# Sparsemax attention: one row of candidates taken before the flag is read, TensorE's candidate rows in another order, and ten rotating rows of kept scores

## The reference

```python
def sparsemax(x):
    x = x - jnp.max(x, axis=-1, keepdims=True)
    zs = -jnp.sort(-x, axis=-1)
    rho = jnp.arange(1, L + 1, dtype=x.dtype)
    cssv = jnp.cumsum(zs, axis=-1) - 1.0
    support = zs > cssv / rho
    k = jnp.maximum(jnp.sum(support, axis=-1, keepdims=True), 1)
    tau = jnp.take_along_axis(cssv, k - 1, axis=-1) / k.astype(x.dtype)
    return jnp.clip(x - tau, 0.0)
```

## Time and profile before

| what | us |
|---|---|
| median of three runs (3720.1 to 3721.49) | 3720.78 |
| the profiled execution | 3726.95 |
| its span | 3725.1 |
| TensorE busy | 2808.6 (75%) |
| VectorE busy | 2231.3 (60%) |
| ScalarE busy | 1432.7 (38%) |
| first to last candidate MAX8, start | 875.5 to 1547.2 |
| first to last probability, start | 959.7 to 1640.6 |

### The profile page before, as it was taken

One profiled execution on the slowest core, in us unless ns is written; L12 is line 12 of the kernel. 1 busy time (PEld: TensorE's weight loads), 2 busy tenths in 40 slices (PEclk: granted clock), 3 DMA queues, 4 the chain that ended last, 5 costly groups with the idle time before them and its releaser, 6 DMA issues. The chain is left out here.

```text
span 3725.1 us, 39786 instructions
## 1 busy us (share of the span) xinstructions
PE 2808.6 (75%) x12862; PEld 1808.0 (49%) x12862; DVE 2231.3 (60%) x4947; ACT 1432.7 (38%) x2218; POOL 329.6 (9%) x145
## 2 busy tenths in 40 slices
PE   2999998354566666667999966888587696699588
PEld 2444445132233333336888844554443685354377
DVE  4666764865777677624555544656564555676377
ACT  2444442212787787732222212222143222166221
POOL 0000000020000000001212202011100110200021
PEclk8999999676777777768999978998888797799799
DMA  1000000024001111001111010000331010522010
GB/s 58 14 8 13 13 8 13 23 74 134 1 23 23 23 24 28 1 10 66 36 48 51 25 48 1 1 0 0 100 75 36 32 45 17 176 69 52 19 46 29
DMA packets 53741, 136.62 MB, mean 37 GB/s; under 512 B 8793, under 2 KB 29281, under 8 KB 48993
## 3 DMA queue, kind: packets, MB, share of 16 engines
q1 hardware_dynamic: 53600, 135.01, 12.2%
HBM read 106.28 MB, written 28.31 MB: 36 GB/s over the span
## 5 line engine op out<-in xcount | busy, mean ns | idle before, releaser
L1675 PE MATMUL ps<-m1e_x_part_s,m1e_up_part_s 128*128 128x512 f32 x1296 | 298.0, 391 | 22.0 <-POOL m1e_up_part_s L1771 15.9
L1445 ACT ACTIVATE l1a_over_s<-l1a_sc_s,l1a_minus_step_s 128x1024 bf16<-128x1024 f32 x256 | 290.0, 1139 | 3.0 <-DVE l1a_minus_step_s L1319 1.7
L1675 PEld LDWEIGHTS ps<-m1e_x_part_s,m1e_up_part_s 128*128 128x128 f32 x1296 | 243.8, 189 | 74.2 <-issue 23.7
L1259 DVE MAX8 l1a_cand_s<-ps 128x8 f32<-128x128 f32 x1024 | 213.0, 281 | 72.0 <-PE ps L1154 68.8
L1187 PE MATMUL ps<-l1a_probs_s,l1h_v_s 128*32 128x256 f32 x1024 | 126.5, 584 | 158.0 <-ACT l1a_probs_s L1453 156.5
L1431 ACT ACTIVATE l1a_sc_s<-ps,l1a_minus_tau_s 128x1024 f32<-128x1024 f32 x128 | 142.0, 1112 | 155.9 <-DVE l1a_minus_tau_s L1288 67.3
L1718 ACT ACTIVATE m1e_act_out_s<-ps 128x512 f32<-128x512 f32 x108 | 64.6, 598 | 346.8 <-PE ps L1675 346.8
L538 DVE TENSOR_SCALAR l0a_probs_s<-l0a_probs_s 128x1024 f32<-128x1024 f32 x128 | 88.4, 691 | 150.3 <-ACT l0a_probs_s L605 149.9
L974 DVE TENSOR_REDUCE l3a_shift_s<-ps 128x1 f32<-128x1024 f32 x128 | 150.3, 1219 | 46.1 <-PE ps L891 46.1
L605 ACT ACTIVATE l0a_probs_s<-ps 128x1024 f32<-128x1024 f32 x128 | 131.1, 1024 | 104.5 <-PE ps L455 103.3
L1154 PE MATMUL ps<-l1h_ka_s,l1h_qa_s 128*128 128x512 f32 x256 | 132.7, 564 | 49.7 <-DVE l1a_cand_s L1259 45.2
(11 more groups left out here) (530 smaller groups left out, 5873.9 us busy)
## 6 DMA issues: line engine op xcount, KB each, us to landing
m1ew_up_s<-m_up SPq DMA_DIRECT2D x9, 1536.0 KB, 6.2
l1h_ka_s<-l_k_parts SPq DMA_DIRECT2D x16, 512.0 KB, 8.0
l3h_ka_s<-l_k_parts SPq DMA_DIRECT2D x16, 512.0 KB, 8.1
m1ew_down_s<-m_down SPq DMA_DIRECT2D x9, 768.0 KB, 4.2
l0a_w_s<-l_w SPq DMA_DIRECT2D x16, 384.0 KB, 2.9
m3ew_up_s<-m_up SPq DMA_DIRECT2D x6, 768.0 KB, 4.2
l1h_qa_s<-l_q_parts SPq DMA_DIRECT2D x16, 256.0 KB, 6.0
l_v_groups<-l1p_v_all_s SPq DMA_DIRECT2D x8, 512.0 KB, 2.9
```

Of the source, the lines that this page charges most:

```text
L1259: ins = nc.vector.max(cand[:, r, 8 * (c + j * 4):8 * (c + j * 4) + 8], ps[:, A0 + f % 2, c * P:(c + 1) * P])
L1445: nc.scalar.activation(over[:, done % 2, :], sc[:, r, :], ACT.Relu, bias=minus_step[:, r:r + 1], accum_out=total[:, i, r:r + 1]).then_inc( ...
L1675: ins = nc.tensor.matmul(ps[:, 2 * (u % 2) + way, :], up_parts[a][:, k, way, c, :], x_parts[b][:, k, half * BANK:(half + 1) * BANK], start ...
```

## The change

Four things change in the stage.

1. **Ten rotating rows of kept scores.** Row r of unit u is kept in row (8u + r) mod 10. Rows 0 and 1 of the next unit then overwrite nothing that the loop behind the flag may read, and ScalarE waits for `settled` only at row 2 (`KEPT - ROWS`).
2. **One row of candidates ahead.** VectorE takes candidate row 0 of unit u + 2 in `settle(u)`, between the last step and the maximum of the worst excesses. So in the next turn rows 1 to 4 stand where rows 0 to 3 stood, and rows 5 to 7 where rows 4 to 7 stood. At the start row 0 of unit 1 is taken behind the first threshold of unit 0.
3. **TensorE's order.** `first_row` moves on by one place to match; row 0 of unit u + 2 stands behind the value products of t = 2.
4. **Three probability buffers instead of four.** A probability waits for the value products three places back.

```diff
+    KEPT = ROWS + 2
+    def kept(u, r):
+
+        return (ROWS * u + r) % KEPT
-        sc = s.sb("sc", [P, ROWS, nk])
+        sc = s.sb("sc", [P, KEPT, nk])
-        probs = s.sb("probs", [P, 4, 2 * NQ])
+        probs = s.sb("probs", [P, 3, 2 * NQ])
...
             for r in range(ROWS):
                 first_row(0, r)
+            first_row(1, 0)
...
                     if u + 1 < UNITS and 2 <= r < 6:
-                        first_row(u + 1, r - 2)
+                        first_row(u + 1, r - 1)
...
-                    if u + 1 < UNITS and t < 4:
-                        first_row(u + 1, 4 + t)
+                    if u + 1 < UNITS and t < 3:
+                        first_row(u + 1, 5 + t)
...
                     if u > 0 and t > 0:
                         value_products(u - 1, t - 1)
+                    if u + 2 < UNITS and t == 3:
+                        first_row(u + 2, 0)
...
                 own.link(nc.vector.tensor_tensor(step[:, :], step[:, :], excess[:, 2, :], ALU.add))
+                if u + 2 < UNITS:
+                    candidates(u + 2, 0)
                 dve.wait_ge(worst_turned, u + 1)
...
             first_threshold(0)
+            candidates(1, 0)
...
-                    for r in range(ROWS // 2):
+                    for r in range(1, 5):
                         candidates(u + 1, r)
                 second_threshold(u)
                 if u + 1 < UNITS:
-                    for r in range(ROWS // 2, ROWS):
+                    for r in range(5, ROWS):
                         candidates(u + 1, r)
...
-                if u > 0:
-                    act.wait_ge(settled, u)
                 for r in range(ROWS):
+                    if u > 0 and r == KEPT - ROWS:
+                        act.wait_ge(settled, u)
                     place = again_place(u, r)
                     act.wait_ge(pair_made, place + 1)
-                    nc.scalar.activation(sc[:, r, :],
+                    nc.scalar.activation(sc[:, kept(u, r), :],
...
-                if NC_ * u + t >= 4:
-                    act.wait_ge(pv_done, NC_ * u + t - 3)
-                nc.scalar.activation(probs[:, t % 4, :],
+                if NC_ * u + t >= 3:
+                    act.wait_ge(pv_done, NC_ * u + t - 2)
+                nc.scalar.activation(probs[:, (NC_ * u + t) % 3, :],
```

More of the change, by code:

```diff
@@ L1187, in value_products @@
                     ins = nc.tensor.matmul(ps[32 * h:32 * h + 32, VALUES, 0:HALF], v[:, n % 2, t, h, :],
-                                           probs[:, t % 4, h * HALF:(h + 1) * HALF],
+                                           probs[:, (NC_ * u + t) % 3, h * HALF:(h + 1) * HALF],
                                            start=(t == 0), stop=(t == NC_ - 1))
@@ L1344, in settle @@
                         for r in range(ROWS):
-                            more.link(nc.vector.tensor_scalar(over[:, 2, :], sc[:, r, :], step[:, r:r + 1], 0.0,
+                            more.link(nc.vector.tensor_scalar(over[:, 2, :], sc[:, kept(u, r), :], step[:, r:r + 1], 0.0,
                                                               ALU.is_gt, ALU.add, accum_out=count[:, r:r + 1]))
-                            more.link(nc.vector.scalar_tensor_tensor(over[:, 2, :], sc[:, r, :], step[:, r:r + 1],
+                            more.link(nc.vector.scalar_tensor_tensor(over[:, 2, :], sc[:, kept(u, r), :], step[:, r:r + 1],
                                                                      zero[:, :].to_broadcast([P, nk]), ALU.subtract, ALU.max,
@@ L1444, in sums @@
                         act.wait_ge(summed, done - 1)
-                    nc.scalar.activation(over[:, done % 2, :], sc[:, r, :], ACT.Relu, bias=minus_step[:, r:r + 1],
+                    nc.scalar.activation(over[:, done % 2, :], sc[:, kept(u, r), :], ACT.Relu, bias=minus_step[:, r:r + 1],
                                          accum_out=total[:, i, r:r + 1]).then_inc(summed, 1)
```

## The result

The changed kernel takes 3685.79 us (median of four runs, 3684.63 to 3688.09), the kernel before on the same chip 3721.14 us. The ratio is 0.9902, 95% interval 0.9885 to 0.9919: 35 us less (30 to 43), 1.0%. I had forecast 3707.2 and a range of 3694 to 3717. The sign was right, the size 2.6 times too small, and the time lies outside the range.

A forecast was written before the change was run, and what follows sets the result against it. The unit-to-unit loop is closed by ScalarE up to the copy, VectorE's flag, then TensorE and VectorE in turn. -13.7 + 1.5 + 0.7 - 2.1 = -13.6 us, from 3720.78 to 3707.2; range 3694 to 3717.

The forecast's parts named there:

- Part 1, the bank: First sums behind the flag: TensorE's 0.91 us wait for row 0's banks goes in 15 units, 13.7 us less.
- One forecast sign: Changed profile: ScalarE's wait for the shift stands in front of row 2, rows 0 and 1 some 2.5 us before.
- Unit 15: Last unit's first sums, without candidate rows, clock 0.50: TensorE paces, so the 0.91 us goes there too.
- Part 2: Candidate row before the worst excess: hidden by VectorE's wait except 0.05 us in 13 units (0.7 us); unit 0 1.5 us late.
- Part 3: TensorE's order and three probability buffers: nothing; bounds 0 and 1.08 us in each of 14 units (15 us).
- Part 4, the clock: TensorE's clock in the first sums behind the shift: 0.15 us off in 14 units, 2.1 us, near no effect.
- 43.4 was forecast: Changed profile: steps of some 43.4 us from shift to shift, against 44.39 before.
- The price of the fast level: First sums behind the shift: 2.4 GHz coming 3 us earlier takes 3.5 rows x 0.40 = 1.4 us off a unit.
- The rival at 3690: First sums: 2.4 GHz comes 3 us earlier in each unit, -11.5 - 14 x 1.4 = -31 us; 13 in 100.
- The slower rival: 1.2 GHz holds through the first sums, 1.1 us more in 14 units: +17 us, 3738; 7 in 100.
- in half the units 3728: Milder case of the slower rival: 1.2 GHz holds through the first sums in half the units, 3728 us.

The follow-up runs named there:

- e2: Changed kernel with eight kept rows, `settled` awaited at row 0 again, candidate row ahead and TensorE's new order kept: 3717.61 us, ratio 0.9987.
- e9: Kernel before with rotating kept rows and three probability buffers alone, nine rows instead of ten, `settled` awaited at row 1: 3698.93 us, ratio 0.9941.
- e3: Kernel before plus six unused 256-column matmuls between the two transposes of `turn`, in TensorE's pause before the shift: 3708.49 us, ratio 0.9968.
- e5: Kernel before plus one needless 0.72 us VectorE operation in each unit, in front of the third threshold: 3719.86 us, ratio 0.9999.
- e11: e8 plus four unused 256-column matmuls in TensorE's pause, and unit 0's candidate row behind the shift: 3665.76 us, ratio 0.9856.
- e8: Changed kernel with three candidate rows in the first sums, eleven rotating rows, `settled` at row 3, TensorE's row 2 between `turn`'s transposes: 3674.28 us, ratio 0.9876.

## Why the prediction was off, step by step

- **Part 1, the bank: right mechanism, size too small.** I took the 0.91 us that TensorE idled in front of row 2, and let row 2 start where the transpose ends. It starts 0.03 behind the transpose's start. What goes is 1.50 - 0.25 = 1.25 us, and at equal clock the first sums are 1.28 shorter at 2.4 GHz (10.89 to 9.61) and 1.3 at the lower clocks (12.27 at 0.72, 10.94 at 0.69). 15 x 1.28 = 19.2 us, not 13.7. One forecast sign failed with it: ScalarE does not wait for the shift in front of row 2, it waits for TensorE's row.
- **Unit 15.** There I had taken 0.91 us off; it was 1.7 (10.13 to 8.43), and a part of that is clock (0.50 to 0.59). At 0.50 nine rows took 8.99 us, 1.1 less than before.
- **Part 2: right.** Unit 0 comes from 1.04 to 2.53 us between `settle` and the worst excess, 1.49 later, as forecast. The Trainium skill's rule in "PSUM — Partial Sum Buffer", section "Engine vs sequencer instructions", that VectorE's queue is strictly first in, first out, agrees with it: the ready flag stood behind the eight MAX8. In the other units nothing sticks out (2.57 to 2.50).
- **Part 3: right.** No new wait shows, and e2, which has part 2 and this one without the rows, moved the time by 1 to 8 us.
- **Part 4, the clock: this step failed.** I took 0.15 us off in 14 units, 2.1 us, "near no effect". By subtraction it was 31.3 - 19.2 = 12.1 us, 0.8 a unit. I reasoned from one unit, as if the fast level came a fixed time behind the shift, whatever TensorE did before. The runs show two things in its place. With TensorE busy in the bank's former wait, 1.2 GHz that begins at the shift is gone 3.1 to 3.7 us behind it instead of 6.6 to 7.2. And the fall left the shift: in six of units 1 to 14 no 1.2 GHz met the first sums, and they took 9.6 to 10.0 us. The three units whose fall stayed at the shift took 10.40 us on average, 1.84 less than before, of which 1.28 is the bank. So as an estimate from these three units (and 10.50 us in six such units of e9), 6 to 8 of the 12 us come from the earlier return, and the rest from where the fall landed. That second part is luck: no row on record tells where the fall would land. The step is 42.16 us, where 43.4 was forecast.
- **The price of the fast level.** 1.4 us a unit is right for 2.4 GHz throughout against the level of the kernel before (e2, e3 and e5: 12.3 to 10.9). For a return 3 us earlier, for which I had worked it out, it is too much: the return 3.4 us earlier was worth about 0.5 us.

The sum as measured: 1.5 (unit 0) - 19.2 (bank) - 12.1 (clock) - 0.9 (the rest) = -30.7 us, the stage in the two profiles; the medians say 30 to 43. The split of the 31.3 us rests on differences at equal clock in single units, not on a run in which the clock was held. The -0.9 is what is left over.

The rival at 3690 had the mechanism, and it got 13 chances in 100 since I asked for 3 us in every unit or nothing. The right form was a mixture: some units at 1.4, some at 0.5 to 0.7, some at 0. That its sum, -31, is the stage's -30.7 is luck: its bank and part 2 (-11.5) are 6.2 us too small, its clock (-19.6) is 7.5 too large. The slower rival (1.2 GHz through the first sums) did not come. Its "in half the units 3728" was added up wrongly, too: 7.7 + 2.2 - 0.9 gives 9 us, 3730; nothing else rests on it.

I used the Trainium skill's "TensorE: Matmul & The Clock Gate", Part 1, for the rule that activity releases the fast state. The trace agrees: once TensorE was busy in what had been the bank's wait, the fast level was back 3.2 us behind the shift and not 6.6. The same part says that the observation of activity runs freely and does not begin with the kernel's work, so that one kernel can meet the level at different places. e5 agrees: a needless 0.72 us moved the fall in 12 of units 2 to 14, and the 11.5 us put in did not show in the time. I had left that sentence out of the sum.

Open: why the level in the kernel before fell with the shift in every unit, and why it does not in the changed kernel. An operation elsewhere in the unit moves the fall at the same step (e5), a fill in front of the shift moves it too (e3), and the new order with its candidate row ahead leaves it in ten units where it was (e2). No kernel here fixes the place of the fall, and none held the clock.

## What to carry over

A freed wait can be worth more than the idle time that the profile shows for it. Here TensorE's row 2 started 0.03 us behind the start of the transpose ahead of it, while that one still ran, so 0.91 us of idle time shown were 1.25 us: count from start to start, not from the end of the instruction. Where a repeated unit meets the slow TensorE level at the same point every time, treat the clock as a term of its own: price one unit at either level, ask whether the change makes TensorE's work behind the fall denser, and put a mixture in the sum. A run with idle TensorE time filled shows that the clock alone has a price (12 us in e3), though not all of it, since the fill may catch only some units.

## What was not expected of the hardware

- 0.72 us more on the path in each of 16 units, at no cost (ratio 0.9999, 0.999 to 1.0008).
- 90 matmuls whose results nothing reads, 0.95 us for six, took 12 us off.
- 1.2 GHz that began within 0.35 us of the shift lasted until 6.6 to 7.2 us behind it in 25 units in which TensorE waited for a bank there, and until 3.1 to 3.7 us in 14 units in which it did not.
- In e11, with the pause in front of the shift filled and a third row ahead, 14 units in a row (2 to 15) ran their first sums at a granted clock of 1.00, 8.8 us each in the 13 that have candidate rows and 6.7 in unit 15. Without the fill (e8) units 2 and 14 had means of 0.57 and 0.58 in the 7 us behind the shift and took 10.1 us. Unit 1 had 0.50 there with the fill and 0.55 without it. The other part of e11, unit 0's candidate row, was not run apart, so that the fill did this is not shown.
